# Attention with split V: low part of V accumulated onto the high part's PSUM columns, the division moved from GpSimd to VectorE, two of sixteen subtractions moved to GpSimd

## The reference, cut to what matters

```python
B, S, D, H, DH = 2, 1024, 128, 16, 64           # S as the drawn input has it
q = l2norm(x @ w_q) * exp(scale)                 # per head
k = l2norm(x @ w_k);  v = x @ w_v
sim  = einsum('bhid,bhjd->bhij', q, k)
attn = softmax(sim)
out  = einsum('bhij,bhjd->bhid', attn, v)
x = layernorm(x + out @ w_out + b_out)
```

## Time and profile before

| what | value |
|---|---|
| median of 3 runs | 1121.53 us |
| the profiled execution's own time | 1121.68 us |
| its span, first to last instruction | 1119.9 us |
| busy: PE, DVE, ACT, POOL | 926.1, 769.4, 772.2, 542.8 us |
| mean granted TensorE clock | 0.928 of 2.4 GHz |

### The profile page before, as it was taken

How to read it: one execution, slowest core, us unless ns; L and a number is a source line. 1 busy time by engine, 2 the same in 40 slices (tenths; PEclk the granted TensorE clock), 3 DMA queues, 4 the chain that set the end, 5 groups by cost and what they waited for, 6 DMA issues and landing times. The chain is left out here.

```text
span 1119.9 us, 31020 instructions
## 1 busy us (share of the span) xinstructions
PE 926.1 (83%) x11628; PEld 848.2 (76%) x11628; DVE 769.4 (69%) x1496; ACT 772.2 (69%) x1276; POOL 542.8 (48%) x481
## 2 busy tenths in 40 slices
PE   3889999999999999999999742999988569899940
PEld 2788988889889888888889732887868458889830
DVE  6699988988998899889989751422349768410202
ACT  5689988988898889988988441433356166587731
POOL 5376755765656557656655136302318253043423
PEclk8799999999999999999999955999998779899975
DMA  8300000000000000000000043112101002023211
GB/s 267 92 2 21 2 2 21 2 2 20 2 20 3 2 20 2 2 21 2 2 21 3 10 170 97 46 54 61 47 25 31 8 25 69 11 61 95 62 51 42
DMA packets 42254, 41.89 MB, mean 37 GB/s; under 512 B 5505, under 2 KB 37249, under 8 KB 41729
## 3 DMA queue, kind: packets, MB, share of 16 engines
q1 hardware_dynamic: 38016, 31.51, 9.3%
q0 software_dynamic: 4096, 8.40, 2.6%
HBM read 25.60 MB, written 14.29 MB: 36 GB/s over the span
## 5 line engine op out<-in xcount | busy, mean ns | idle before, releaser
L645 DVE TENSOR_TENSOR Pl<-Pr 128x1024 f16<-128x1024 f32 x256 | 325.5, 1293 | 45.8 <-ACT Pr L548 44.4
L548 ACT ACTIVATE Pr<-SC,cur_nesc,cur_esc 128x1024 f32<-128x1024 f32 x256 | 308.8, 1209 | 28.6 <-issue 10.4
L409 PE MATMUL SC<-QK 128*128 128x256 f16 x1024 | 238.9, 274 | 1.0 <-ACT QK L530 1.0
L410 PE MATMUL SC<-QK 128*128 128x256 f16 x1024 | 238.9, 274 | 0.0
L435 PE MATMUL OP<-V,Pr 128*128 128x129 f16 x2048 | 212.0, 220 | 9.4 <-DVE osum L666 9.4
L437 PE MATMUL OP<-V,Pl 128*128 128x65 f16 x2048 | 205.3, 192 | 0.0
L435 PEld LDWEIGHTS OP<-V,Pr 128*128 128x128 bf16 x2048 | 183.9, 97 | 16.4 <-issue 13.6
L757 POOL TENSOR_TENSOR Ob<-osum,rden 128x128 f32<-128x128 f32 x128 | 133.4, 1042 | 109.7 <-DVE osum L666 109.0
L437 PEld LDWEIGHTS OP<-V,Pl 128*128 128x128 f16 x2048 | 180.9, 97 | 2.7
L1663 POOL DMA_INDIRECT yg<-ys,slots x64 | 74.8, 1169 | 145.7 <-DMA ys<-yb 63.0
L1161 PE MATMUL DB<-wd,hid 128*128 (+1 forms) x864 | 125.9, 290 | 12.1 <-DVE x L1495 6.7
(11 more groups left out here) (189 smaller groups left out, 2083.2 us busy)
## 6 DMA issues: line engine op xcount, KB each, us to landing
ys<-yb SPq DMA_DIRECT2D x92, 64.0 KB
xg<-xs SPq DMA_DIRECT2D x12, 384.0 KB, 4.5
wst<-in_up SPq DMA_DIRECT2D x8, 512.0 KB
xs<-zero SPq DMA_DIRECT2D x2, 1472.0 KB
scratch<-in_up SPq DMA_DIRECT2D x1, 2304.0 KB, 8.6
wd<-in_wd SPq DMA_DIRECT2D x1, 2304.0 KB, 13.7
wd<-in_wd SPq DMA_DIRECT2D x1, 2048.0 KB
QK<-in_wqkv SPq DMA_DIRECT2D x4, 384.0 KB, 7.3
```

Of the source, the lines that this page charges most:

```text
L409: eng.matmul(out, QK[:, b, 1, key:key + P], rhs, start=True, stop=False)
L410: mm = eng.matmul(out, QK[:, b, 2, key:key + P], rhs, start=False, stop=True)
L548: eng.activation(Pr[:, n % PB, :, :], SC[s % 2][:, :, :], ACT.Exp, bias=cur_nesc[:, b:b + 1], scale=cur_esc[:, b:b + 1]).then_inc(s_exps, 1)
L645: eng.tensor_tensor(Pl[:, n % PB, :, :].rearrange("p a b -> p (a b)"), pr, high(pr)[:, 1::2], ALU.subtract).then_inc(s_low_probs, 1)
```

## The change

`av` makes three matmuls where it made two: high probabilities with V's high part and ones (65 columns), high probabilities with V's low part (64 columns) into the same PSUM columns, low probabilities with the high part (65). `read_out` on DVE takes the reciprocal, waits for it, and multiplies straight from PSUM into `Ob`; `osum`, its reduction, and POOL's `divide` are gone. `low_probs` of slots 1 and 15 of each head runs on POOL, in front of what POOL has in that slot. The tables move several steps.

```diff
+POOL_LO = (1, 15)
-VALUE_AT = (1, 4, 9, 15)
-VALUE_LOW_AT = (1, 4, 10, 15)
+VALUE_AT = (2, 4, 6, 10)
+VALUE_LOW_AT = (5, 8, 13, 15)
-TURN_AT = (6, 8, 9, 10, 11, 12, 13, 14)
-OUT_TURN_AT = (24, 28, 31, 32, 35, 36, 37, 41)
-OUT_AT = (41, 44, 46, 50, 58, 60, 62, 63)
+TURN_AT = (6, 7, 9, 10, 11, 12, 13, 14)
+OUT_TURN_AT = (24, 25, 31, 32, 35, 36, 37, 40)
+OUT_AT = (41, 44, 47, 50, 57, 59, 61, 63)
...
-                wait(eng, s_low_probs, n + 1)
+                pool = s in POOL_LO
+                wait(eng, s_low_probs_pool if pool else s_low_probs, low_count(n, pool))
...
-                    wait(eng, s_inverse_sums, 16 * i + 8 * b + u - 1)
-                    wait(eng, s_av_read, 16 * i + 8 * b + u - 1)
+                    wait(eng, s_outputs, 16 * i + 8 * b + u - 1)
...
-                        at = VW * r
+                        at = (DH + 1) * r
-                        eng.matmul(OP[u % 2][:, at:at + 129], hi, V[:, b, tile, 0:129],
+                        eng.matmul(OP[u % 2][:, at:at + 65], hi, V[:, b, tile, 0:65],
                                    start=first, stop=False, skip_group_check=True)
+                        eng.matmul(OP[u % 2][:, at:at + 64], hi, V[:, b, tile, 65:129],
+                                   start=False, stop=False, skip_group_check=True)
...
-                wait(eng, s_outputs, m - 1)
-                eng.reciprocal(rden[:, u % 4, :], OP[u % 2][:, DH:DH + VW + 1:VW]).then_inc(s_inverse_sums, 1)
-                parts = OP[u % 2][:, 0:2 * VW].rearrange("p (r k c) -> p r c k", r=2, k=2)[:, :, 0:DH, :]
-                eng.tensor_reduce(osum[:, u % 2, :, :], parts, AX, ALU.add).then_inc(s_av_read, 1)
+                wait(eng, s_outputs, m - 3)
+                eng.reciprocal(rden[:, u % 4, :], OP[u % 2][:, DH:2 * DH + 2:DH + 1]).then_inc(s_inverse_sums, 1)
+                wait(eng, s_inverse_sums, m + 1)
+                o = OP[u % 2][:, 0:2 * DH + 2].rearrange("p (r c) -> p r c", r=2)
+                eng.tensor_tensor(Ob[:, 2 * u:2 * u + 2, DH * b:DH * b + DH], o[:, :, 0:DH],
+                                  rden[:, u % 4, :].unsqueeze(2).to_broadcast([P, 2, DH]), ALU.mult).then_inc(
+                                      s_outputs, 1)
...
-                if not ended(i):
+                if not ended(i) and sh not in POOL_LO:
                     low_probs(i, s)
...
+            def low_probs(i, s):
+                n = 32 * i + s
+                wait(eng, s_exps, n + 1)
+                wait(eng, s_av_products, n - PB + 1)
+                pr = Pr[:, n % PB, :, :].rearrange("p a b -> p (a b)")
+                eng.tensor_tensor(Pl[:, n % PB, :, :].rearrange("p a b -> p (a b)"), pr, high(pr)[:, 1::2],
+                                  ALU.subtract).then_inc(s_low_probs_pool, 1)
...
+                if not ended(i) and sh in POOL_LO:
+                    low_probs(i, s)
```

More of the change, by code:

```diff
@@ L56, with low_count @@
 RESIDUAL_AT = 14
+POOL_LO = (1, 15)
 GROUP_AT = (0, 3, 5, 7)
 SUM_AT = (1, 4, 6, 8)
-VALUE_AT = (1, 4, 9, 15)
-VALUE_LOW_AT = (1, 4, 10, 15)
+VALUE_AT = (2, 4, 6, 10)
+VALUE_LOW_AT = (5, 8, 13, 15)
 NORM_AT = (4, 6, 8, 10)
-TURN_AT = (6, 8, 9, 10, 11, 12, 13, 14)
-OUT_TURN_AT = (24, 28, 31, 32, 35, 36, 37, 41)
-OUT_AT = (41, 44, 46, 50, 58, 60, 62, 63)
+TURN_AT = (6, 7, 9, 10, 11, 12, 13, 14)
+OUT_TURN_AT = (24, 25, 31, 32, 35, 36, 37, 40)
+OUT_AT = (41, 44, 47, 50, 57, 59, 61, 63)
 UP_HIGH_AT = (18, 26)
 UP_LOW_AT = (20, 28)
+def low_count(n, pool):
+    mine = [k for k in range(SLOTS) if (k in POOL_LO) == pool]
+    return n // SLOTS * len(mine) + sum(k <= n % SLOTS for k in mine)
 def proj_slot(j):
@@ L231, in attention @@
         rden = sb("rden", [P, 4, 2], F32)
-        osum = sb("osum", [P, 2, 2, DH], F32)
         Ob = sb("Ob", [P, NT, 2 * DH], F32)
@@ L261, in attention @@
         s_low_probs = sem("s_low_probs")
+        s_low_probs_pool = sem("s_low_probs_pool")
         s_av_products = sem("s_av_products")
-        s_av_read = sem("s_av_read")
         s_inverse_sums = sem("s_inverse_sums")
@@ L749, in _ @@
         def _(eng):
-            def divide(i, s):
-                b, u = s // SLOTS, s % SLOTS // 2
-                m = 16 * i + 8 * b + u
-                wait(eng, s_av_read, m + 1)
-                wait(eng, s_inverse_sums, m + 1)
-                eng.tensor_tensor(Ob[:, 2 * u:2 * u + 2, DH * b:DH * b + DH], osum[:, u % 2, :, :],
-                                  rden[:, u % 4, :].unsqueeze(2).to_broadcast([P, 2, DH]), ALU.mult).then_inc(
-                                      s_outputs, 1)
+            def low_probs(i, s):
[5 more added lines that the diff above has]
+                                  ALU.subtract).then_inc(s_low_probs_pool, 1)
             def inverse_norms(h, hb, g):
@@ L792, in slot @@
                 h, sh = 2 * i + s // SLOTS, s % SLOTS
+                if not ended(i) and sh in POOL_LO:
+                    low_probs(i, s)
                 if prepares(i, s):
                     prepare(h + 1, (s // SLOTS + 1) % 2, sh)
-                if s % 2 == 0:
-                    if s >= 4 and not ended(i):
-                        divide(i, s - 4)
-                    elif s < 4 and started(i, 1):
-                        divide(i - 1, s + 2 * SLOTS - 4)
             for m in (t["ident16"], t["ident32"]):
```

## The result

| what | before | after |
|---|---|---|
| median | 1120.98 us (4 runs, 1119.92 to 1121.6) | 1104.66 us (4 runs, 1103.79 to 1107.37) |
| ratio, 95% interval | | 0.9859 [0.9839, 0.988] |
| span of the profiled execution | 1119.9 us | 1105.5 us |
| end of the last exponentials of attention | 629.6 us | 611.7 us |

The change saves 16.3 us in the median. The forecast was 22.5 us by the medians (1098.5), its range 1082 to 1115.

What follows compares the result with a forecast made beforehand. PE was taken as the limit, with gaps mostly set by a late DVE. Terms of -3.35 us for each of six full pairs, -20.1, with first pair, last and tail made -23.1: 1098.5 us, range 1082 to 1115.

Steps and rivals of the forecast that it cites:

- the likeliest case: Whole kernel: the forecast's own case, 1088 to 1106 us, chance 0.48.
- parts 1, 2 and 5: Step tables: V's copy earlier for the exponentials -1.15, output products apart -0.7 and -0.85, transposes moved 0 us a pair.
- parts 3, 4, 6 and 7: Divisions off POOL -0.6 and -0.45, read-out 0, eight more matmuls per `av` +0.4, two subtractions on POOL 0 us a pair.
- The copy of V: Slots 2 and 18: copy behind the exponentials, which start 1.2 us earlier; PE's slot 19 wait shrinks, -1.15 us a pair.
- Output products apart: Slot 14's gap goes, -0.7 us a pair; slot 31's product waits for slot 29's add, -0.85.
- Divisions off POOL: DVE's normalisations and POOL's divisions stop delaying each other before slots 13 and 27: -0.6 and -0.45 us a pair.
- Read-out: DVE's multiplication from PSUM, 0.27 us, replaces the reduction at 0.40 us with reciprocal; no change counted, bounds 0.3 and 0.5.
- Transposes moved: Two of three M1 bank collisions go, 1.1 us of PE gaps a pair; counted nothing since DVE is late next.
- Eight more matmuls: `av`: 3 ns per further matmul, 90 ns a triple, 0.8 us a pair, half where DVE sets the pace: +0.4.
- Two subtractions on POOL: Slots 1 and 15: 2.2 us each on POOL, upper bound 4.3, covered by DVE's idle 2.9 us a head; costed at nothing.
- First pair and the end: First pair has no output products, -1.5 us; POOL's division leaves the tail of attention, -0.5 us.
- DVE paces more than I think: Rival: PE's gaps move to the next late-DVE place, output products and divisions worth half; 1109 us, chance 0.2.

Runs made afterwards that it cites:

- spread products: The changed kernel with output products at least three slots apart and the out-transposes moved in front of them: 1104.99 us, ratio 0.9857.
- the low part first: The changed kernel with the product with V's low part put first in each tile of `av`: 1110.37 us, one run.

## Why the prediction was right, and where it was off

Direction and range held, and the likeliest case was the right one, with 16.3 of the 22.5 us. The mechanism was right in kind: PE's waits for a late DVE closed, 4.1 us a pair where 3.75 were forecast. How the gain splits was not: by its parts 1, 2 and 5 the tables had -2.7 a pair and bring -1.0 alone or, on top of the rest, -1.1; parts 3, 4, 6 and 7 had -0.65 and bring -1.6. That the errors went against one another, and the sum came nearer than its parts, is luck. Step by step:

- **The copy of V (-1.15 a pair).** Right: the wait of slot 19 is 0.27 us in after, and alone the move takes it from 1.4 to 0.35 and the pair down by 1.4. The wait of ACT for PE is gone from the table of waits.
- **Output products apart (-0.7 and -0.85).** The waits of slots 14 and 31 are gone, as forecast, but the tables can't be credited with all of it: with the old tables in the changed kernel that of slot 14 is gone too and that of slot 31 down to 0.7. The price paid for it was only partly seen. "The products of slots 27 and 29 each follow an add of two slots before, and DVE is late there": they wait 0.7 and 0.4, within the 0.85 net. But the product moved from slot 14 to 15 puts an add in front of the projection of slot 16, and there the step was blind: 1.2 us a pair, had POOL not taken the subtraction of that slot.
- **Divisions off POOL (-0.6 and -0.45).** Right in kind, and smaller than what DVE gained. "Three such places lie between slot 4 and the read-out" and "two or three before slot 27" counted only where PE waits; over all of DVE's work it is 1.1 us a head, 2.3 a pair, with the old tables. The new places of V's low part take the normalisations' share of it, 0.6 us a head, back, which the prediction did not see. By the Trainium skill, "SBUF — State Buffer", section "Who interferes with whom", the lock is held for the whole instruction; the trace agrees, with POOL's 1.90 us inside DVE's 4.08 for 2.35.
- **Read-out (0).** Nearly right: 0.27 was estimated for the multiplication, 292 ns measured; the read-out is 0.16 to 0.25 us a head shorter.
- **Transposes moved (0).** The waits at slots 9 and 28 are gone, and one of 0.4 stands at slot 25. It needs the division off POOL (1.8 us in its place otherwise).
- **Eight more matmuls (+0.4).** This is the step that failed in the sum. 90 ns a tile were forecast, 92.2 measured: (92.2 - 87.1) x 8 x 32 = 1.3 us a pair. And "half of it where DVE sets the pace" was wrong, all of it shows: waits fell by 4.1 us a pair, the pair by 2.7. The terms of the waits sum to 3.75, close to the 4.1; this one cost 0.9 more than its place in the sum, 5.4 us in six pairs. By the Trainium skill, "TensorE: Matmul & The Clock Gate", section "LDWEIGHTS (loading the stationary operand)", with 107 ns a load, the further loads would have cost 219 us if nothing covered them, an estimate; the trace does not agree, with 92 ns for three loads and matmuls.
- **Two subtractions on POOL (0).** The duration was right, 1.90 us against 2.2, and the cover by DVE's idle time too: with the old tables they change nothing. DVE's idle time in all grew from 3.2 to 4.4 us a head. The zero was wrong in company. With the new tables they are worth 6.6 us, by freeing DVE's queue in front of the add of slot 15 and not by load.
- **First pair and the end.** -1.5 was forecast for the first pair, 0.35 came: its two heads take 33.4 and 37.3 us, before 33.8 and 37.3, from exponentials to exponentials. For the end -0.5 was forecast. In the profiled execution it got 3.7 us longer, 23.9 us instead of 20.2 from the last exponentials to the first matmul of the mixture. That part is the clock, below. The three executions that are 2.0 to 3.6 us faster may be those in which it is shorter; they left no trace.

So for the six pairs -16.4 stands against -20.1, and the rest is first pair, end and an earlier start. Of the rivals, "DVE paces more than I think" was true in its words (PE's waits did move on to where DVE is late) at 3.1 us of waits left, though its 1109 was too high.

## What to carry to other kernels

On an engine that works in order, put the short instruction that another engine waits for ahead of the long one of the same slot; here that exchange, with POOL's two subtractions taken back, brought some 10 us more where the whole change had brought 16. Test two parts of a change as a square of four kernels, since a part costed at nothing may be what another part stands on, as POOL's subtractions were for the new tables. Compare them by the stage that was changed and not by the total alone: the tables alone lost more than half of their 6 us again, in a trace with more time at the lower clock. And count the lock between two engines over all their work, both ways, not at the places where somebody is seen to wait.

## What the runs showed of the hardware that was not expected

**The clock at the end of attention.** The granted clock in the windows view (columns as above), first of after behind its last exponentials (611.7), then of before behind its own (629.6):

```profile
611.70:616.50 4.80, 3.45 (x80) 2.87 (x77) 1.78 (x10) 1.39 (x4) 3.03 (x8) 1.00 0.00 0
```

```profile
616.50:622.00 5.50, 3.41 (x14) 2.85 (x15) 1.14 (x6) 2.37 (x5) 0.00 (x0) 0.52 0.01 3
```

```profile
629.70:645.00 15.30, 8.28 (x92) 6.96 (x90) 8.85 (x37) 3.60 (x9) 2.94 (x11) 1.00 0.10 22
```

In after it falls to 0.52, the level of 1.2 GHz, while the last out-transposes and output products still run; in before it stays at 1.00 until they are done. In both, each of the last out-transposes stands alone between waits of 0.67 us. The products' matmuls start 0.21 us apart instead of 0.11. Over the traces of this study the way from the last exponentials to the mixture is 20.2 us before, 23.9 after, 20.6 to 23.0 in the others, so this is a spread of up to 3.7 us that no edit here was aimed at. The clock had fallen elsewhere behind a single wait of PE (1.87 us with spread products, 2.54 us with the low part first); here there is no such wait in front of the fall, only several of 0.67. In the 4.80 us before the fall PE was busy for 3.45; in before it was busy for 8.28 of 15.30 and kept the clock. These sums don't tell why the one fell and the other did not.

**POOL's long subtraction.** 1895 ns for 1024 columns against 1153 for 512, 1.45 ns for each further column, where 1.96 was taken from 128 and 512: the 2.2 forecast was somewhat high, and its upper bound of 4.3 us far off.

**Three short matmuls.** A third load and matmul in a tile adds 5 ns; of the three distances 29.3, 33.6 and 29.3 ns the odd one stays without a cause.
